# Routing three token tiles ahead of the fourth, with two weight low parts on GpSimd

## The reference, cut to what matters

```
x = x + cross_attention(layernorm(x), context, mask)      # 16 heads, 1601 keys per batch, q, k and v with biases
h = layernorm(x); q = h @ Wq.T
x = x + (q @ h.T) @ h                                     # per batch, no softmax
h = layernorm(x)
logits = h @ gate_w + gate_b                              # 8 experts
top_v, top_i = top_k(logits, 2);  w = softmax(top_v)
for e in range(8):
    x = x + cw[:, e] * (relu(h @ w1[e] + b1[e]) @ w2[e] + b2[e])     # w1: 512 x 2048, w2: 2048 x 512
```

## Time and profile before

| | us |
|---|---|
| Median of 3 runs | 1276.45 |
| Lowest and highest run | 1275.84 and 1281.73 |
| Profiled execution, device time | 1274.77 |
| Its span | 1273.0 |
| TensorE busy (matmul) | 1240.2 |
| VectorE busy | 842.6 |
| ScalarE busy | 673.7 |
| GpSimd busy | 160.2 |

### The profile page before, as it was taken

One profiled execution on the slowest core, in us unless ns is written; L12 is line 12 of the kernel. 1 busy time (PEld: TensorE's weight loads), 2 busy tenths in 40 slices (PEclk: granted clock), 3 DMA queues, 4 the chain that ended last, 5 costly groups with the idle time before them and its releaser, 6 DMA issues.

```text
span 1273.0 us, 22180 instructions
## 1 busy us (share of the span) xinstructions
PE 1240.2 (97%) x8497; PEld 1155.5 (91%) x8497; DVE 842.6 (66%) x2192; ACT 673.7 (53%) x1194; POOL 160.2 (13%) x86
## 2 busy tenths in 40 slices
PE   7999999999999999999999999999979999999997
PEld 5799999999999999999999999989768989889896
DVE  4565666566565666656566655676767787877877
ACT  5345544645544553554455446444544767677673
POOL 2203100300400130040022004000031000000012
PEclk9999999999999999999999999999989999999999
DMA  9002200220220030022004002200327777676763
GB/s 333 28 1 88 84 1 1 94 78 1 92 80 1 17 124 32 1 92 80 1 28 144 1 1 92 97 1 1 104 83 245 238 237 263 229 250 240 240 218 110
DMA packets 61506, 129.04 MB, mean 101 GB/s; under 512 B 3572, under 2 KB 21120, under 8 KB 61160
## 3 DMA queue, kind: packets, MB, share of 16 engines
q1 hardware_dynamic: 59240, 120.85, 27.5%
q0 software_dynamic: 2176, 6.95, 1.7%
HBM read 121.89 MB, written 15.34 MB: 108 GB/s over the span
## 4 chain that ended last, share of the span: by engine, by line
PE 92%; DVE 4%; ACT 2%; DMA 1%; issue 1%; POOL 0%; SPq 0%; POOLq 0%; DVEq 0%
PE ptp L837 24%; PE work L837 20%; PE work L1136 8%; PE pv L982 7%; PE ptp L966 7%; PE work L875 6%; PE work L1138 4%; PE ptp L1157 2%; PE ptp L1158 2%; PE ptp L1160 2%; PE ptp L1159 2%; PE ptp L1161 2%; PE work L844 1%; DMA raw<-in_ctxT 1%; DVE pt L1387 1%; ACT pt L578 1%
## 5 line engine op out<-in xcount | busy, mean ns | idle before, releaser
L837 PE MATMUL ptp<-vw_hi,cx_hi 128*128 128x256 f32 x832 | 241.8, 291 | 0.0
L837 PE MATMUL ptp<-vw_lo,cx_hi 128*128 128x256 f32 x832 | 235.4, 283 | 0.0
L837 PE MATMUL ptp<-vw_hi,cx_lo 128*128 128x256 f32 x832 | 235.3, 283 | 0.0
L518 POOL TENSOR_TENSOR cx_lo<-raw,cx_hi 128x1664 fp32r<-128x1664 f32 x30 | 113.7, 3789 | 666.0 <-ACT cx_hi L578 666.0
L837 PE MATMUL work<-cx_hi,kw_hi 128*128 128x400 f32 (+1 forms) x504 | 175.4, 348 | 3.0 <-POOL cx_lo L518 1.7
L837 PEld LDWEIGHTS ptp<-vw_hi,cx_hi 128*128 128x128 f32 x832 | 159.2, 191 | 17.0 <-issue 17.0
L837 PE MATMUL work<-cx_hi,kw_lo 128*128 128x400 f32 (+1 forms) x504 | 173.7, 345 | 0.0
L837 PE MATMUL work<-cx_lo,kw_hi 128*128 128x400 f32 (+1 forms) x504 | 173.2, 344 | 0.0
L1387 DVE TENSOR_TENSOR pt<-ptp,pt 128x512 fp32r<-128x512 f32 (+1 forms) x224 | 141.1, 649 | 33.9 <-ACT pt L578 30.4
L1296 DVE SCALAR_TENSOR_TENSOR kk_lo<-work,biasT,kk_hi 128x400 fp32r<-128x400 f32 (+1 forms) x128 | 78.9, 632 | 122.5 <-ACT kk_hi L591 121.9
L837 PEld LDWEIGHTS ptp<-vw_hi,cx_lo 128*128 128x128 f32 x832 | 159.3, 191 | 0.0
(11 more groups left out here) (262 smaller groups left out, 2373.2 us busy)
## 6 DMA issues: line engine op xcount, KB each, us to landing
w1raw<-in_w SPq DMA_DIRECT2D x32, 1024.0 KB, 5.1
w2raw<-in_w SPq DMA_DIRECT2D x32, 1024.0 KB, 6.5
raw<-in_ctxT SPq DMA_DIRECT2D x31, 832.0 KB, 6.4
pr<-in_mask SPq DMA_DIRECT2D x8, 800.5 KB, 4.5
xrow<-x_rows SPq DMA_DIRECT2D x7, 256.0 KB, 6.2
y_rows<-y_out_rows POOLq DMA_DIRECT2D x7, 256.0 KB, 2.5
xin<-in_x SPq DMA_DIRECT2D x1, 1024.0 KB, 8.9
qwraw<-in_qwT SPq DMA_DIRECT2D x1, 1024.0 KB, 11.0
```

Of the source, the lines that this page charges most:

```text
L518: pool.tensor_tensor(cx[1][:, :, sl], raw[:, k % 2], cx[0][:, :, sl].bitcast(F32), ALU.subtract).then_inc(c_lo, 1)
L837: last = pe.matmul(dst, lhs(i, c), rhs(j, c), start=(c == 0 and (i, j) == (0, 0)), stop=(c == n - 1 and (i, j) == (1, 0)))
```

## The change

Five edits:

- In the last batch the residual and statistics of a tile become a step r of their own, one key later than its scaling. The row weights of tiles 0 to 2 move up to the value step (v, 0, 1). Step l keeps only the small steps and the root and moves behind key 4; the three normalising instructions become steps m in the second half.
- The logits of tiles 0 to 2 get a signal of their own, and tile 3's go to another bank.
- `choose` and `picks` run for tiles 0 to 2 and then for tile 3. TensorE counts and gathers tiles 0 and 1, counts for tile 3, and gathers tiles 2 and 3. The gather loops over tiles first. Both of its signals now come within tile 3's part, and the totals are taken after it.
- The low parts of w1 piece 1 and w2 piece 0 go to GpSimd, ahead of those of xn. The second waits for ScalarE's copy named q1 (gT of tile 3).
- VectorE splits the gathered tokens right behind the row numbers.

```diff
-        steps += s[0] + v[0:2] + s[1] + e[0:1] + v[2:3] + e[1:2] + v[3:4] + s[2] + v[4:6] + s[3]
         if h and last:
+            norms = [("m", 0, j) for j in range(EARLY)]
+            steps += s[0] + v[0:1] + norms[0:1] + v[1:2] + s[1] + e[0:1] + v[2:3] + norms[1:2] + e[1:2] + v[3:4]
+            steps += norms[2:] + s[2] + v[4:6] + s[3]
...
-            steps += k[:1] + a[:1] + k[1:2] + a[1:2] + k[2:3] + a[2:] + k[3:4] + [("l", 0, 0)] + k[4:5]
+            steps += k[:1] + a[:1] + k[1:2] + r[:1] + a[1:2] + k[2:3] + r[1:2] + a[2:] + k[3:4] + r[2:] + k[4:5] + [("l", 0, 0)]
...
# GpSimd, ahead of the low parts of xn
+            pool.wait_ge(w1_hi, 2)
+            pool.wait_ge(w1_lo, 1)
+            pool.tensor_tensor(w1s[1][:, 1], w1raw[:, 1], w1s[0][:, 1].bitcast(F32), ALU.subtract).then_inc(w1_lo, 1)
+            pool.wait_ge(m_out, copied("q1"))
+            pool.wait_ge(w2_hi, 1)
+            pool.tensor_tensor(w2s[1][:, 0], w2raw[:, 0], w2s[0][:, 0].bitcast(F32), ALU.subtract).then_inc(w2_lo, 1)
...
# TensorE
+            def gather(t):
+                pe.wait_ge(x_lo, t + 1)
+                pe.wait_ge(pick_done, t + 1)
+                for c in range(C):
+                    dst = yb[2 + c // 2][:, (c % 2) * SLOTS:(c % 2 + 1) * SLOTS]
+                    for i in range(2):
+                        last = pe.matmul(dst, xn[i][:, t, c * P:(c + 1) * P], pick[:, t],
+                                         start=(t == 0 and i == 0 and c % 2 == 0), stop=(t == TT - 1 and i == 1 and c % 2 == 1))
+                    if c % 2 and t == TT - 1:
+                        last.then_inc(xg_full, 1)
...
+            earlier_tokens(range(EARLY), work[1])
+            gather(0)
+            gather(1)
+            pe.wait_ge(chosen_done, 2)
+            earlier_tokens(range(EARLY, TT), work[2])
+            gather(2)
+            gather(3)
...
# VectorE, last batch
+                    if last and step == ("v", 0, 1):
+                        row_weights(range(EARLY))
+                    if kind == "r":
+                        dve.wait_ge(w_free, count(b, last, ("a", 0, j)))
                         dve.wait_ge(vb_done, TT)
-                        row_weights(range(EARLY))
+                        residual(j)
                     if kind == "l":
-                        layer_norm(xs, hn, ln2, 2, range(EARLY))
+                        norm_weights(2, range(EARLY))
+                    if kind == "m":
+                        normed(xs, hn, ln2, j)
...
# VectorE, middle (choose and picks are the old lines for the tiles given)
+            choose(range(EARLY), work[0], "logits0")
+            picks(range(EARLY), work[1], "earlier0", 1)
+            choose(range(EARLY, TT), yb[1], "logits1")
+            dve.tensor_tensor(wts[:, 0], top8[:, :, 1], top8[:, :, 0], ALU.subtract).then_inc(gate_diff, 1)
+            picks(range(EARLY, TT), work[2], "earlier1", 2)
...
             dve.tensor_copy(row_i[:], row_f[:]).then_inc(rows_done, 1)
-            w1_part(0, 1)
-
+            gathered(0)
...
-            gathered(0)
             dve.wait_ge(m_full, filled("total"))
...
-            w2_part(0, 0)
+            dve.wait_ge(w1_lo, 2)
+            dve.wait_ge(w2_lo, 1)
             experts(0)
```

More of the change, by code:

```diff
@@ L103 @@
 FILLED = (["q0_1", "att3", "b1", "q0_2", "q0_3", "turn0_3", "pre0", "pre1", "pre2", "own0", "own1", "own2", "q1", "pre3",
-           "own3", "turn1_0", "turn1_1", "turn1_2", "turn1_3", "logits", "earlier", "total", "places", "weights",
+           "own3", "turn1_0", "turn1_1", "turn1_2", "logits0", "turn1_3", "logits1", "earlier0", "earlier1", "total", "places", "weights",
            "b2_0", "b2_1", "b2_2", "b2_3"])
@@ L1022, in logits @@
                 pe.wait_ge(m_out, copied(f"turn1_{t}"))
-                return plain(work[0][:, t * E:(t + 1) * E], lambda c: hT[:, c, t * P:(t + 1) * P], lambda c: gw[:, c])
+                bank = work[0] if t < EARLY else yb[1]
+                return plain(bank[:, t * E:(t + 1) * E], lambda c: hT[:, c, t * P:(t + 1) * P], lambda c: gw[:, c])
             pe.wait_ge(w_free, count(LASTB, 1, ITEMS[1][-1]))
@@ L1055, in _ @@
             for t in range(EARLY):
-                logits(t)
+                last = logits(t)
+            last.then_inc(m_full, 1)
             pe.wait_ge(ln2, TT + EARLY + 1)
@@ L1059, in _, with earlier_tokens @@
             logits(EARLY).then_inc(m_full, 1)
+            def earlier_tokens(ts, bank):
+                for t in ts:
+                    for u in range(t + 1):
+                        last = pe.matmul(bank[:, t * E:(t + 1) * E], (before if u == t else ones16)[:], chosen[:, u],
+                                         start=(u == 0), stop=(u == t))
+                last.then_inc(m_full, 1)
+            def gather(t):
[8 more added lines that the diff above has]
+                        last.then_inc(xg_full, 1)
             pe.wait_ge(zeroed, 7)
             pe.wait_ge(chosen_done, 1)
[L1062 to L1066, removed]
+            earlier_tokens(range(EARLY), work[1])
[5 more added lines that the diff above has]
+            gather(3)
             for t in range(TT):
@@ L1070, in _ @@
             last.then_inc(m_full, 1)
[L1072 to L1082, removed]
             def turn_tokens(n):
@@ L1243, in statistics, with norm_weights @@
                 join()
[L1245 removed]
+            def norm_weights(o, ts):
                 for t in ts:
@@ L1355, in item @@
                 elif kind == "a":
-                    done = count(b, last, step)
-                    dve.wait_ge(w_full, done)
+                    dve.wait_ge(w_full, count(b, last, step))
                     scaled(k, bank).then_inc(w_free, 1)
-                    dve.wait_ge(w_free, done)
-                    residual(k)
                 elif kind == "n":
@@ new lines, in picks @@
+            def picks(ts, bank, name, done):
+                r = slice(ts[0], ts[-1] + 1)
+                dve.wait_ge(m_full, filled(name))
+                dve.wait_ge(chosen_done, done)
+                dve.scalar_tensor_tensor(out=place[:, r, 0:E],
+                                         in0=bank[:, ts[0] * E:(ts[-1] + 1) * E].rearrange("p (t e) -> p t e", e=E),
+                                         scalar=1.0, in1=chosen[:, r], op0=ALU.add, op1=ALU.mult).then_inc(place_done, 1)
+                dve.wait_ge(place_done, done)
+                for t in ts:
+                    dve.tensor_scalar(pick[:, t], iota_s[:], place[:, t, 0:1], None, ALU.is_equal).then_inc(pick_done, 1)
```

62 lines of the change are left out of this document (27 added, 35 removed).

## The result

The changed kernel takes 1281.31 us (median of 20 runs, 1276.80 to 1282.99) and the kernel before 1276.32 (20 runs, 1274.84 to 1281.73): ratio 1.0034, 95% interval 1.0026 to 1.0041. By that ratio it is 4.3 us slower (the medians lie 5.0 apart), where 4.1 was forecast, and it is inside the 0.5% that was called no change. The two profiled executions lie further apart than the medians: 1274.77 and 1282.41, which is 7.6 us.

A forecast was written before the change was run, and what follows sets the result against it. TensorE's chain of waits was taken to bound the kernel, with time won only where it idles or runs at its lower clock. A gather 6.7 us late less 2.6 gained made 4.1 slower, 1280.5 us; range 1270.5 to 1283.0.

The forecast's parts named there:

- Place: TensorE idles at the end of the last batch's first half, and from late norms to the first expert's hidden layer.
- Part 1: Last batch's residuals and norms moved: TensorE's stalls of 1.15 and 1.59 us shrink; 2.6 us gained, bounds 1.2 and 2.9.
- Part 3, the port: GpSimd's 4.6 us second low part holds VectorE's norms of tiles 0 to 2 out of SBUF: 4.46 us lost.
- rival 1: The norms of tiles 0 to 2 pass GpSimd's subtraction: 6.1 us faster, 1270.3; chance 0.2.
- The clock under the logits: After TensorE's 5.4 us pause the lower clock lasts until the gather: 5.16 us of work takes 10.0.
- Rival 2: Norms blocked, but the clock stays up or recovers under self values and transposes: in the middle 0.9 us faster, 1275.5; chance 0.27.
- Part 2: Tiles 0 to 2 routed first, so the gather starts earlier: taken alone 3.5 us gained, between 1.9 and 5.3.
- Rival 3: The clock does not return within the gather, slowing it and hidden matmuls: 7.0 us slower, 1283.4; chance 0.08.
- The sum: Gather ends 6.7 us late, less 2.6 from the last batch's moved residuals and norms: 4.1 us slower, 1280.5; chance 0.45.
- part 2's reading of that row: The first indirect transfer took 2.97 us instead of 0.97 while VectorE ran a 2.28 us low part.

The follow-up runs named there:

- e2: The kernel before with only the new order of residuals, norm weights and norms of the last batch; ratio 0.9971 to the kernel before, median 1274.2 us.
- e3: The kernel before with only the two low parts of w1 and w2 moved to GpSimd; ratio 1.0054 to the kernel before, median 1284.7 us.
- e11: The change with tile 3's choice and counts ahead of the first gather, so four gathers run unbroken; ratio 1.0004 to the kernel before, 1277.8 us.
- e1: The change with the w2 low part back on VectorE at its old place; ratio 0.9979 to the kernel before, median 1275.3 us.
- e10: e1 with three of tile 3's four small count matmuls ahead of the first gather, one left in the break; ratio 0.9984 to the kernel before, 1275.7 us.
- e4: The change with five unused fp32 filler matmuls while TensorE waits for the norms; ratio 1.0014 to the kernel before, median 1279.0 us.
- e6: e1 with the wait for tile 3's choice and its counts one gather later; ratio 0.9982 to the kernel before, median 1276.2 us.
- e8: e2 with the low part of w1 piece 1 on GpSimd instead of VectorE; ratio 0.9980 to the kernel before, median 1274.7 us.
- e9: e1 with tile 3's choice and counts ahead of the first gather, so four gathers run unbroken; ratio 0.9955 to the kernel before, 1271.9 us.

## Why the prediction was right, point by point

**Place.** Both places where TensorE stood still were the places where the time moved.

**Part 1** held. Both stalls went as worked out: none ahead of the fourth key product, 0.43 us of 1.59 left. Forecast 2.6 us; the traces have 2.60, and the ratio of e2 has 3.7 with an interval that takes in 2.6.

**Part 3, the port** held in kind and size. GpSimd took 4.50 us where 4.6 was forecast, and held the chain for 4.35 where 4.46 was forecast (the product went from 0.16 to 4.51). What was caught was the product, which stands ahead of the norms, and not the norms; e3 showed that the norms are caught too, so rival 1 would have failed either way. The Trainium skill (SBUF — State Buffer, "Who interferes with whom") has this rule: the second of the two to issue waits for the whole instruction of the first. The traces agree, with 4.51, 5.53 and 2.36 us of VectorE work against 4.50, 4.54 and 2.35 of GpSimd's. The one row that stands apart is e3's product, which starts 0.01 us behind the subtraction and yet took 0.16 us.

**The clock under the logits** was the first mis-sized term. It fell in the pause, as forecast (the change's windows have 0.97 from 935 to 936 and 0.50 from 936 on), but was back at 942.8 and not at the gather. The 5.16 us of the kernel before, from the last self values to the end of the logits of tiles 0 to 2, had been forecast to take 10.0; they took 7.5 (937.60 to 945.13). From TensorE's resumption to the first gather matmul 14.3 us were forecast (939.8 to 954.1); 11.7 were measured (937.60 to 949.34). The step that failed reads "I take the lower level until the gather": it rested on the one pattern that the rows held. Rival 2, which had the clock recover under self values and transposes, was nearer; in e11 it did so, at 941.0. But the forecast's pattern occurs as well. In e3, after a pause of 5.04 us, the clock stood at 0.50 from 936.7 to 964.0, and the 24 logits matmuls took 5.13 us:

```profile
945.12 5.13 PE L850 MATMUL work<-gw,hT 128*128 128x8 f32 x24
...
947.00:948.00 1.00, 1.00 (x7) 1.00 (x6) 0.00 (x0) 0.00 (x0) 0.00 (x0) 0.50 0.00 0
```

What decides between the two was not tried.

**Part 2** was the second, and here the sign of the working was wrong. The forecast took the clock back within the gather. The gather had been priced with its break only as 0.35 us of lost time, and it was not asked what the break does to the clock. From the first gather matmul to the first hidden one 7.4 us were forecast (6.1 and 1.26); 8.6 were measured, and 5.3 us of the hidden layer at half rate cost 2.6 more. Rival 3 named just this, the clock not back within the gather, with a chance of 0.08, but gave no cause that would bring it about; e1, without the long pause, shows it as well.

**The sum** came out by luck. By the traces 2.6 us too much under the logits stood against 3.8 too little in gather and hidden layer. A third term was put at nothing: the second stretch at the lower clock, under the first expert's output, lasted 6.8 us in the change (973.5 to 980.3) where it had lasted 3.4 before, worth up to 1.7 us. Together that would make the change some 7 us slower, and the two traced executions do lie 7.6 apart. The medians lie 5.0 apart and the ratio says 4.3: the trace of the kernel before lies 1.5 us under its median, and that of the change 1.1 us over its own. By the ratios, the steps from kernel to kernel are: part 1, −3.7; parts 2 and w1, e1 less e2, +1.0; the second low part, the change less e1, +7.0. They lead to +4.3 by the way they are formed, which is no check. The prediction had −2.6, −3.5 and, as what its sum leaves for the third, +10.2. A time that falls inside the range says little of the terms behind it.

## What to carry to other kernels

Work that is moved to an idle GpSimd is not off the path: find out what VectorE runs beside it, and if that is an SBUF to SBUF instruction or one with two SBUF inputs on the critical chain, charge the whole length of GpSimd's instruction, however small VectorE's is. Filling TensorE's wait with the next stage's first half can give back all that it gains, where it puts a short break into the run of matmuls under which the clock came back; compare the time from the start of that run to the return of the clock, in the rows of both kernels, before the start times. The best version here chooses three tiles early but gathers all four in one run, and leaves the large subtraction on VectorE: 0.9955 and 0.9960 of the kernel before.

## What the runs showed of the hardware that was not expected

- One 8-column matmul between 192-column ones, 0.1 us, went with a return of the clock at 13.5 us (e10). The eight traces with an unbroken gather had 3.7 to 6.6, five of the six with a broken one 13.1 to 14.5, and the sixth, e4, 3.6. In e4 the gather and its break are those of e1, so something ahead of the gather has a part in it. Why the break puts off the return is open.
- The clock rose under the 24 logits matmuls of 8 columns in the change (0.87 over 942 to 945) and ahead of them in e11 (1.00 over 941 to 944), and in both fell again after them, at 946.2 and 944.4. So a fall in an idle stretch need not last until the next long run of wide matmuls; in e3 it did.
- The pause of 0.95 to 0.97 us, over which the clock had stood at 1.00, went with a fall in others: in e2 the granted clock was 0.50 from 933.8 to 937.2 (in e6 from 933.9 to 937.3), and the last self values took 1.96 us instead of 1.12. It cost 0.8 us there in one row, and what decides it was not tried. Its row in e2:

```profile
933.66 1.96 PE L1022 MATMUL ptp<-hn,pre 128*128 128x512 f32 x2 [0.95 <-DVE pre L1496]
```

- Small VectorE work is caught elsewhere too: in the change the 0.19 us sum that makes the choice took 1.30 us, from the start of GpSimd's low part of tile 3 to its end. It cost nothing, since the counts that wait for it stand behind tile 3's logits, which end at 948.19 (946.31 + 1.88).

```profile
946.85 1.28 POOL L562 TENSOR_TENSOR xn_lo<-hn,xn_hi 128x512 fp32r<-128x512 f32 x1 [6.10 <-ACT xn_hi L587]
946.86 1.30 DVE L1545 TENSOR_TENSOR chosen<-best 128x24 bf16<-128x24 f32 x1
```

- The first indirect transfer took 2.97 us beside VectorE's subtraction and takes 1.22 in the change without it, so part 2's reading of that row held:

```profile
955.03 1.22 POOL L568 DMA_INDIRECT x_rows<-hn,row_i  x1 [6.90 <-DVE row_i L1710]
```

- The second stretch at the lower clock, under the first expert's output, lasted 3.4 us in seven of the eight traces with an unbroken gather (all but e8) and 6.8 us in all six with a broken one and in e8, which is up to 1.7 us of their times. So it goes with the break; whether the break causes it was not tried. It also means that the ratios of e9 and e11 may hold this gain beside that of the earlier return.
